# The lane one-hots of an expert dispatch: one VectorE instruction for eight tiles, tiles innermost

## The reference, cut to what matters

```python
x = x + 0.5 * ffn(layernorm(x))        # first phase
x = x + attention(layernorm(x))
x = x + 0.5 * ffn(layernorm(x))        # second phase, same weights

def ffn(x):                            # 2048 tokens of 256, 8 experts, 2 per token
    probs = softmax(x @ Wg);  gate_vals, expert_idx = top_k(probs, 2)
    oh = one_hot(expert_idx.reshape(-1), 8)
    pos = sum((cumsum(oh) - 1) * oh)   # place of the pair within its expert
    kept = pos < 640                   # an expert takes 640 pairs at most
    # dispatch_mask[e, pos] = which pair;  rows gathered, relu(x w1) w2, scattered back by gate
```

## Time and profile before

| what | us |
|---|---|
| median of 3 runs | 839.33 |
| lowest and highest of them | 833.71, 839.90 |
| the profiled execution, whole | 837.06 |
| its span, first to last instruction | 835.3 |
| around the span | 1.8 |
| TensorE busy | 766.1 (92%) |
| VectorE busy | 443.1 (53%) |
| GpSimd busy | 310.9 (37%) |

### The profile page before, as it was taken

How to read it: one execution, slowest core, us unless ns; L and a number is a source line. 1 busy time by engine, 2 the same in 40 slices (tenths; PEclk the granted TensorE clock), 3 DMA queues, 4 the chain that set the end, 5 groups by cost and what they waited for, 6 DMA issues and landing times. The chain is left out here.

```text
span 835.3 us, 15880 instructions
## 1 busy us (share of the span) xinstructions
PE 766.1 (92%) x6126; PEld 670.3 (80%) x6126; DVE 443.1 (53%) x848; ACT 366.2 (44%) x611; POOL 310.9 (37%) x363
## 2 busy tenths in 40 slices
PE   5789999999999987898998998886899999999997
PEld 3469999999999965565665664645799999999997
DVE  7766345544634225777677674259446345444530
ACT  3215445534534301456546556231246345544631
POOL 3154554463434252232132122102734544464133
PEclk9999999999999997799999999897999999999999
DMA  9424543354242144012222110070542652454122
GB/s 330 127 71 135 155 130 86 101 149 121 51 121 26 15 113 152 36 47 79 78 80 105 57 51 3 26 228 3 185 110 64 159 127 62 129 138 108 38 25 25
DMA packets 60070, 80.27 MB, mean 96 GB/s; under 512 B 11140, under 2 KB 46980, under 8 KB 59988
## 3 DMA queue, kind: packets, MB, share of 16 engines
q1 hardware_dynamic: 44660, 60.35, 21.6%
q0 software_dynamic: 15360, 19.23, 12.6%
HBM read 51.72 MB, written 19.01 MB: 85 GB/s over the span
## 5 line engine op out<-in xcount | busy, mean ns | idle before, releaser
L610 DVE SCALAR_TENSOR_TENSOR second_h_lo<-second_ps_h,second_h_hi 128x320 fp32r<-128x320 f32 x128 | 62.9, 492 | 104.5 <-ACT second_h_hi L469 104.5
L610 DVE SCALAR_TENSOR_TENSOR first_h_lo<-first_ps_h,first_h_hi 128x320 fp32r<-128x320 f32 x128 | 62.9, 492 | 104.5 <-ACT first_h_hi L469 104.5
L386 POOL DMA_INDIRECT after_first<-first_scaled,first_add_now x40 | 69.6, 1740 | 115.2 <-ACT first_scaled L462 112.0
L386 POOL DMA_INDIRECT out_dram<-second_scaled,second_add_now x40 | 69.2, 1729 | 115.5 <-ACT second_scaled L462 112.9
L1104 DVE TENSOR_REDUCE at_maxima<-at_ps_front 128x4 f32<-128x512 f32 (+2 forms) x96 | 96.8, 1039 | 20.9 <-PE at_ps_front L1232 20.7
L986 POOL TENSOR_SCALAR_AFFINE_SELECT at_probs<-at_probs 128x512 f32<-128x512 f32 x64 | 39.9, 635 | 142.4 <-ACT at_probs L1044 142.4
L721 PE MATMUL second_ps_o<-second_w_hi,second_h_hi 128*128 128x256 f32 x320 | 91.2, 285 | 0.0
L721 PE MATMUL first_ps_o<-first_w_hi,first_h_hi 128*128 128x256 f32 x320 | 91.1, 285 | 0.0
L721 PE MATMUL second_ps_o<-second_w_lo,second_h_hi 128*128 128x256 f32 x320 | 90.0, 281 | 0.0
L721 PE MATMUL second_ps_o<-second_w_hi,second_h_lo 128*128 128x256 f32 x320 | 90.0, 281 | 0.0
L721 PE MATMUL first_ps_o<-first_w_hi,first_h_lo 128*128 128x256 f32 x320 | 89.9, 281 | 0.0
(11 more groups left out here) (271 smaller groups left out, 1751.8 us busy)
## 6 DMA issues: line engine op xcount, KB each, us to landing
first_w_raw<-in_L_ffn_w_dram SPq DMA_DIRECT2D x16, 1024.0 KB, 8.7
second_w_raw<-in_L_ffn_w_dram SPq DMA_DIRECT2D x16, 1024.0 KB, 6.6
at_q_stack<-at_pre_hi SPq DMA_DIRECT2D x16, 256.0 KB, 2.5
at_k_stack<-at_pre_hi SPq DMA_DIRECT2D x16, 256.0 KB, 2.5
x<-_attn_hidden_states_dram SPq DMA_DIRECT2D x4, 512.0 KB, 6.0
normed_rows<-first_xn SPq DMA_DIRECT2D x4, 512.0 KB, 7.0
x<-after_first SPq DMA_DIRECT2D x4, 512.0 KB, 6.1
at_q_stack<-at_pre_lo SPq DMA_DIRECT2D x8, 256.0 KB, 2.8
```

What stands on the lines that cost most here:

```text
L386: pool.indirect_dma_start(sum_rows, bass.IndirectOffsetOnAxis(ap=add_now[par][:, s:s + 1], axis=0), scaled[par][:, s, :], None, bounds_che ...
L610: v.scalar_tensor_tensor(h_lo[:, f, a * HALF:(a + 1) * HALF], ps_h[:, f % 2, a, 0:HALF], 0.0, h_hi[:, f, a * HALF:(a + 1) * HALF].bitcast( ...
```

## The change

The table of lanes gets a third dimension: each lane number is repeated eight times, 1,024 elements in each partition in place of 128. The lane numbers of the pairs are written in float16 (`in_tile_h`) where they were float32. The lane one-hots of a part are made by one `tensor_tensor` of 1,024 elements in place of eight `tensor_scalar` of 128; it compares the repeated table with the eight numbers of the part, broadcast over the lanes. In its output the pair tile is the innermost dimension, so that the 128 lanes of one pair tile lie eight elements (16 bytes) apart, and with that step TensorE reads its stationary operand. `lane_ready` counts parts, not tiles. Each partition holds 1,792 bytes more of table.

```diff
--- before.py
+++ after.py
@@ -59,7 +59,7 @@
         self.identity_bf = sb("identity_bf", [P, P], BF16)
         self.earlier = sb("earlier", [P, P], BF16)
         self.ones = sb("ones", [P, P], BF16)
-        self.lane = sb("lane", [P, P], F16)
+        self.lane = sb("lane", [P, P, E], F16)
         self.slot_tile = sb("slot_tile", [P, LC])
         self.rank = sb("rank", [P, E])
         self.first_tile = sb("first_tile", [P, E])
@@ -78,7 +78,7 @@
                              (self.not_first, 1.0), (self.pick, 0.0), (self.hide_half, 0.0), (self.hide_half_t, 0.0)):
             pool.memset(table[:], value).then_inc(self.filled, 1)
         small = dict(allow_small_or_imprecise_dtypes=True)
-        pool.iota(self.lane[:], [[1, P]], base=0, channel_multiplier=0, **small).then_inc(self.filled, 1)
+        pool.iota(self.lane[:], [[1, P], [0, E]], base=0, channel_multiplier=0, **small).then_inc(self.filled, 1)
         pool.iota(self.slot_tile[:], [[1, LC]], base=0, channel_multiplier=0, **small).then_inc(self.filled, 1)
         pool.iota(self.rank[:], [[-1, E]], base=E, channel_multiplier=0, **small).then_inc(self.filled, 1)
         pool.iota(self.first_tile[:], [[ST, E]], base=0, channel_multiplier=0, **small).then_inc(self.filled, 1)
@@ -268,11 +268,11 @@
             position = eb("position", [P, K * T])
             column = eb("column", [P, K * T])
             tile_no = eb("tile_no", [P, K * T])
-            in_tile = eb("in_tile", [P, K * T])
             numbers = eb("numbers", [P, LC])
             of_tile = eb("of_tile", [P, K * T, LC], F16)
             tokens_of = eb("tokens_of", [P, K * T, LC], F16)
-            of_lane = eb("of_lane", [P, K * T, P], F16)
+            in_tile_h = eb("in_tile_h", [P, K * T], F16)
+            of_lane = eb("of_lane", [P, K * T // E, P, E], F16)
         h_hi = sb("h_hi", [P, FT, CAP], F32R)
         h_lo = sb("h_lo", [P, FT, CAP], F32R)
         w1_hi.append(sb("w1_hi1", [P, DK, FF], F32R))
@@ -566,14 +566,14 @@
                   v.tensor_tensor(column[:], column[:], over[:], ALU.add))
             for a in range(3, ST):
                 chain(v.scalar_tensor_tensor(tile_no[:], position[:], float(a * P), tile_no[:], ALU.is_ge, ALU.add))
-            chain(v.scalar_tensor_tensor(in_tile[:], tile_no[:], -float(P), position[:], ALU.mult, ALU.add),
+            chain(v.scalar_tensor_tensor(in_tile_h[:], tile_no[:], -float(P), position[:], ALU.mult, ALU.add),
                   v.tensor_tensor(column[:], column[:], tile_no[:], ALU.add))
-            for n in range(K * T):
-                if n % PART == 0:
-                    part = slice(n, n + PART)
-                    v.tensor_tensor(of_tile[:, part], const.slot_tile[:].unsqueeze(1).broadcast_to([P, PART, LC]),
-                                    column[:, part].unsqueeze(2).broadcast_to([P, PART, LC]), ALU.is_equal).then_inc(tiles_ready, 1)
-                v.tensor_scalar(of_lane[:, n, :], const.lane[:], in_tile[:, n:n + 1], None, ALU.is_equal).then_inc(lane_ready, 1)
+            for h in range(PARTS):
+                part = slice(h * PART, (h + 1) * PART)
+                v.tensor_tensor(of_tile[:, part], const.slot_tile[:].unsqueeze(1).broadcast_to([P, PART, LC]),
+                                column[:, part].unsqueeze(2).broadcast_to([P, PART, LC]), ALU.is_equal).then_inc(tiles_ready, 1)
+                v.tensor_tensor(of_lane[:, h], const.lane[:], in_tile_h[:, part].unsqueeze(1).broadcast_to([P, P, PART]),
+                                ALU.is_equal).then_inc(lane_ready, 1)
 
             v.wait_ge(list_made, 1)
             v.tensor_scalar(gather_index[:], ps_x[:, 1, 0:LC], -1.0, 0.0, ALU.add, ALU.max).then_inc(rows_listed, 1)
@@ -674,8 +674,8 @@
             for n in range(K * T):
                 if n % PART == 0:
                     pe.wait_ge(tokens_ready, n // PART + 1)
-                pe.wait_ge(lane_ready, n + 1)
-                last = pe.matmul(ps_x[:, 1, 0:LC], of_lane[:, n, :], tokens_of[:, n, :], start=(n == 0), stop=(n == K * T - 1))
+                    pe.wait_ge(lane_ready, n // PART + 1)
+                last = pe.matmul(ps_x[:, 1, 0:LC], of_lane[:, n // PART, :, n % PART], tokens_of[:, n, :], start=(n == 0), stop=(n == K * T - 1))
                 if n % PART == PART - 1 and n < K * T - 1:
                     spin(pe, const, ps_o[:, 0, :], 8)
             last.then_inc(list_made, 1)
```

## The result

| | before | after |
|---|---|---|
| median of 20 runs each | 837.34 | 834.67 |
| lowest and highest | 833.71, 839.90 | 832.47, 837.06 |
| the profiled execution's span | 835.3 | 830.7 |
| second phase, `of_tile` to the end of the list | 9.32 | 8.05 |
| first phase, the same | 9.30 | 7.70 |

The ratio of the times is 0.9976, with a 95% interval of 0.9965 to 0.9988: the kernel after is 1.0 to 2.9 us faster. That is a gain that can be told from nothing with this many runs, and it lies within the 1% that the prediction took for no change. Both stretches that the change touches are shorter, by 1.60 and 1.27 us, 2.87 in sum.

What follows compares the result with a forecast made beforehand. VectorE (2.24 us a part) and TensorE (2.25) were taken to bound the list together; 0.5 saved in the second phase and 0.9 in the first made 1.4, so 835.7 by profile, 837.9 by median, middle 836.8, range 832.0 to 842.3.

Steps and rivals of the forecast that it cites:

- Who was the bound before: In the list stage, a part takes VectorE 2.24 us and TensorE 2.25; the two arrive together.
- The comparison, 0.83: VectorE's new 1,024-element instruction takes 0.83 us, bounds 0.69 and 1.22; rival at float32 pace, 1.22, chance 0.10.
- GpSimd waits for the comparison, VectorE for GpSimd: Shared way into SBUF: first list matmul 1.94 us after `of_tile`, a part 1.88; rival without GpSimd's wait, chance 0.12.
- Bursts of 0.54: Eight list matmuls on TensorE, no longer paced by lanes, take 0.54 us; the stationary operand's step costs nothing.
- slow stepped load: Rival: TensorE's bursts take 1.6 us at low clock, 0.86 at full; kernel 2.4 later, 840.6; chance 0.22.
- The prediction's other reading: A skill page lists stepped columns among those TensorE's fast weight load takes, which would leave a burst at 0.54 us.
- The clock rises at the same time: Second phase: clock 0.50 up to 580.60 us as before, so the third spin takes 1.28.
- the clock as a rival: Clock rises at another time: one spin more or less at low clock moves a phase 0.85 us; chance 0.05.
- Nothing behind the list absorbs it: Indices, GpSimd's copy and gathers hang on the list alone, so the 1.4 us saved reaches the end.
- The table: At the start, the longer iota costs 0.8 to 0.9 us more, covered by 1.15; 0.7 at most at twice that.
- Time outside the stages: Sign of being wrong: time moves outside the two phases, or they differ from before by over 2 us in sum.

Runs made afterwards that it cites:

- four executions: Profiled executions with the kernel after's stage: that kernel twice, with its table filled last, and with the 60 spins replaced by stepped loads; stages save 2.9, 2.7, 2.1, 1.9 us.
- the other order of dimensions: The kernel after with lanes innermost, pair numbers broadcast along the innermost dimension, and packed columns for TensorE: 835.6 us, ratio 0.9979.
- The ladder: The kernel after with the 60 spins behind the list replaced by six groups of 16 matmuls, steps 1 to 32 elements: 833.95 us in a single run.

## Why the prediction was right, and what in it was mis-sized

The verdict of the forecast holds: no change over 1%, the time (834.67) inside the range of 832.0 to 842.3, the direction right. The size was about half: 1.4 us from the stages, where the medians differ by 2.7 and the stages by 1.9 to 2.9 in four executions. Of the 2.1 us by which 836.8 was too high, 0.9 is the base: it stands on 836.8 + 1.4 = 838.2, taken from three runs and one profile, and twenty runs have 837.34. The steps one by one, by the profiled pair:

- **Who was the bound before.** Right. VectorE's 2.24 and TensorE's 2.25 arrived together, and without the spins the kernel before keeps its stage (9.36).
- **The comparison, 0.83.** Mis-sized. It takes 0.68 to 0.69, the lower bound. The 0.65 ns an element came from the spacing of instructions of 128 elements; with the same fixed 0.15 it is (0.69 - 0.15)/1,024 = 0.52. The Trainium skill (VectorE: DVE Perf Modes, "The perf-mode tier table") gave an estimated 0.69 and the trace agrees. For the other order of dimensions 1.22 was right, the upper bound.
- **GpSimd waits for the comparison, VectorE for GpSimd.** Right in kind: `tokens_of` 1.10, the next `of_tile` 1.01, and both back at 0.48 where GpSimd is not used. The first list matmul was put at 1.94 and came at 1.73, a part at 1.88 and came at 1.53. By the timeline of the kernel after the comparison ends at 570.69, `tokens_of` at 571.26 (0.57 later, counted as 0.65), and the next comparison starts at 571.53 (0.27 later, counted as 0.40). With 0.14 of the comparison that is 0.35 a part; at the first list matmul 0.14 + 0.08 of it count, worth 0.2 in each phase. The rest lies behind the spins.
- **Bursts of 0.54.** The sum came out close (second phase 2.04 against 2.16, first phase 2.02) and the reason given for it was wrong: that was luck. "Only the step differs from the loads of rows 6, so I take 0.54" took the step as costing nothing. The ladder has it at 0.060 in place of 0.025 a pair, and the packed burst is 0.2 shorter. The 0.54 was no price of packed loads, since those bursts still waited for lanes; it happened to be above that of stepped ones. The rival "slow stepped load" was right in kind; at 0.06 a pair it stayed below the 0.12 from which it would have decided. The prediction's other reading, that a fast load of stepped columns leaves the 0.54 untouched, has the size but not the mechanism.
- **The clock rises at the same time.** Not so in this pair, and there it is the largest term. It rose 4.8 us after the first list matmul in the second phase, at 576.1, where the old time after `of_tile` was 577.3: the third spin took 0.88 in place of the 1.28 of the forecast. In the first phase the first spin went partly at the full clock and took 1.37 from the end of its burst to its own, in place of 1.71:

```profile
37.55 0.49 DVE L573 TENSOR_TENSOR first_of_tile<-slot_tile,first_column 128x320 f16<-128x320 f32 x1
...
39.81 1.52 PE L197 MATMUL first_ps_o<-pick,ones 128*128 128x256 bf16 x8
...
44.63 0.62 PE L678 MATMUL first_ps_x<-first_tokens_of,first_of_lane 128*128 128x40 f16 x8
```

The four executions with this stage have 0.88, 1.14, 1.22 and 1.50 for that third spin, so the forecast's 1.28 lies in the middle of a scatter and one profile could not have given it. The prediction had the clock as a rival at 0.05, too low a chance for what every execution shows in some degree.
- **The sum of these.** Second phase: 0.21 (start) + 0.12 (bursts) + 0.40 (spins) = 0.73 on top of the 0.52 forecast: 1.25. First phase: 0.21 + 0.14 + 0.33 = 0.68 on top of 0.92: 1.60. Nothing is left over in this pair. What repeats in every execution is the start and the bursts, 0.7 us in both phases; it takes the 1.4 to 2.1, against the 2.4 that the four executions have in the mean.
- **Nothing behind the list absorbs it.** Right: from the end of the list to the first expert matmul of the second phase it is 596.1 - 582.2 = 13.9 us before and 591.5 - 577.6 = 13.9 after.
- **The table.** The iota takes 1.94 where 1.1 was said, 1.70 more than before against a cover of 1.15, and moves the transposes by 0.37, which the prediction said it would not; an element took twice what was reckoned, the case for which it named 0.7 at most. Nothing was lost by it: the kernel before with this iota keeps its time and its `of_tile`. What stands behind the transposes, the second ten spins, took 1.25 in place of 2.34 in this execution; in the others with this table at this place it took 1.25 to 2.25.
- **Time outside the stages.** The warning "or if time moves outside them" came true in the profiled pair (1.2 us over the attention). The kernel before and after differ there by less than the same kernel does from one execution to another (236.5 and 237.9).

## What to carry to other kernels

When two engines arrive together at every hand-over, taking work from one shows only what it held up in the other; name the next bound and take that too, here the fillers written for the old pace, which were worth 1.7 to 2.7 us of stage time beside the 1.9 to 2.9 of the change. An operand layout moves cost between engines: price it on both sides, the writer's pace (0.69 or 1.22) and the reader's (0.060 or 0.025 a pair), before choosing. A small product handed to GpSimd in the middle of VectorE's stream costs its own time and a turn on each side: 1.10 us here, where VectorE did it in 0.48. And a single pair of profiles has one draw of the moment at which the clock rises: compare stages over several executions before giving each term its size.

## What the runs showed of the hardware

- A load of 128 columns with a 40-column matmul takes 0.025 us a pair at the full clock with steps of one and two elements of float16, 0.034 with four, 0.060 with eight, and 0.063 at 16 and 32 (one execution, the same in both phases). In the chain the burst of eight with a step of eight takes 0.45 at a granted clock of 0.50 and 0.45 to 0.47 at 1.00, so its price does not go with the clock.
- A float16 `tensor_tensor` of 1,024 elements takes 0.69 with an operand broadcast over a middle dimension and 1.22 with both broadcast and the number constant along the innermost one.
- GpSimd's iota costs 0.24 for 128 elements, 1.19 for 512 and 1.94 for 1,024: 1.9 ns an element, twice the slope between its 8 and 128 elements. Issued behind the other tables the same 1,024 took 1.62.
- Beside a GpSimd iota two instructions of four elements on VectorE, a `tensor_scalar` and a `reciprocal`, took 0.53 and 0.46 in place of 0.17 and ended when it did (one execution).
- The granted clock rose from 0.50 to 1.00 6.4 us after the first list matmul in the kernel before, 4.8, 5.4, 5.6 and 6.1 in four executions with the stage of the kernel after, and 4.9 in the one with two comparisons of four tiles (second phase each). In the first phase of the kernel after it was 1.00 at the first burst and fell to 0.50 during the first spins, at 40.2.
